# Tiles of every 64th node in a two-layer graph attention kernel, with eight columns to take out the diagonal

## The chip, the core and the metric

The kernel runs on one core of a Trainium2 chip. The metric is the device time of one execution in microseconds (us). "Before" is the kernel ahead of the change, "after" the kernel behind it. Engines: TensorE (PE), VectorE (DVE), ScalarE (ACT), GpSimd (POOL), and SyncE (SP), which here only issues DMAs. The core's 16 DMA engines move all data between DRAM and SBUF.

## The reference

There are N = 8192 nodes with D = 128 features each, and an adjacency matrix of 8192 x 8192 int32 (256 MiB) that holds the diagonal and some 8 other neighbours in a row.

```python
h = jnp.maximum(_layernorm(x), 0.0)
x = x + _L0_gnn_ref(h, adj, W, a)
h = jnp.maximum(_layernorm(x), 0.0)
x = x + _L1_gnn_ref(h, adj, Wq, bq, Wk, bk, Wv, bv)
...
# layer 0: s1 = (h@W)@a1, s2 = (h@W)@a2; e = leaky_relu(s1[:, None] + s2[None, :], 0.2)
#          out = elu(softmax(where(adj > 0, e, -9e15)) @ (h@W))
# layer 1: q, k, v = h@Wq.T+bq, h@Wk.T+bk, h@Wv.T+bv
#          out = elu(softmax(where(adj > 0, q@k.T/sqrt(128), -9e15)) @ v)
```

## The kernel before

The nodes are cut into T = 64 tiles of P = 128 nodes, one node for each SBUF partition. Tile t holds nodes 128 t to 128 t + 127. Each layer visits the tiles in turn.

**Start.** SP issues four loads of x (L445, 16 tiles each), the weights, and then adjacency tiles 0 and 1. ACT issues a load of the 8192 diagonal elements (L1169). DVE builds constants (L614 to L637), PE mixes weights (L1340 to L1346), DVE takes the statistics of all 64 tiles of x (L662), and during the first three tiles ACT, PE and DVE compute the projected rows h@W. POOL writes them, two tiles at a time, to a DRAM table, `table0` (L561).

**Layer 0 (`survey`).** For each tile, SP loads four quarters of 128 rows x 2048 columns (`load_adj`, L448), 1 MiB each, into one of two buffers. A quarter of tile t + 2 is issued when ACT has read the same quarter of tile t. ACT turns int32 into a bf16 mask (`read_quarter`, L1176). PE packs the 8192 columns into 512 PSUM columns with 16 matmuls, one for each segment of 512 columns, each by a multiple of the identity, `shifted[:, s, :]`, that holds 64 * 2^s (`pack`, L1354). `pack_end` takes out the node itself (L1360): in a tile of 128 nodes in a row, the diagonal elements lie in 128 neighbouring columns of one segment, and a 128 x 128 matrix `off_diag`, made by DVE's `hide_diag` (L637), is added there. DVE reads neighbours out of the packed sums (`extract`, L702), lists them (L761), and POOL gathers the neighbours' rows from `table0` with nine indirect DMAs for each tile (L574). A tile's own rows come by `load_self` (L461). Four to seven tiles later DVE and PE form scores, softmax and sums; the input of layer 1 is staged, and SP writes it four tiles at a time to `table1` (L482).

**Layer 1 (`attend`).** It does not read the adjacency again. For each tile, SP loads its own rows (L522), POOL gathers nine times from `table1` (L605), and SP writes `out` four tiles at a time (L515).

Engines run their instructions in program order and wait on semaphores. A branch that handles inputs which the lists can't hold is not taken.

Of the kernel before, what the change touches and what calls it, by code (L numbers as in the profile page):

```python
# [5 lines left out]
P = 128  # L6
# [35 lines left out]
def two_layer_graph_attention(nc, x, adj, W, a, Wq, bq, Wk, bk, Wv, bv, out):  # L42
# [15 lines left out]
    x_tiles = x.rearrange("(t p) d -> p t d", p=P)  # L58
    out_tiles = out.rearrange("(t p) d -> p t d", p=P)
# [3 lines left out]
    table1 = nc.dram_tensor("table1", [N + 1, D], F32, kind="Internal").ap()  # L63

    with ExitStack() as ctx:
# [111 lines left out]
        off_diag = place([2, P], BF16)  # L177
# [265 lines left out]
        def _(sp):  # L443
# [3 lines left out]
            def load_adj(tile, k, q):  # L447
                sp.dma_start(adj_sb[:, k, q, :], adj[bass.ds(tile * P, P), q * QUARTER:(q + 1) * QUARTER])\  # L448
                  .then_inc(adj_in[k][q], 16)
# [10 lines left out]
            def load_self(v, k):  # L460
                sp.dma_start(Gt[:, k, 0, :], table0[bass.ds(v * P + 1, P), :]).then_inc(self_in[k], 16)  # L461

            def load_group(g):
                for b in range(GROUP):
                    s = g * GROUP + b
                    if live(s, -2):
                        for q in range(QUARTERS):

                            sp.wait_ge(mask_done, QUARTERS * s + q + 1)
                            load_adj(s + 2, b % 2, q)  # L470
                    if isinstance(s, int) and s == 5:
                        sp.wait_ge(zeros_in, 32)
                        for k in range(4):
                            sp.wait_ge(table0_in[k], 16 * UNITS // 4)
                        load_self(0, 0)
                    if not isinstance(s, int) or 5 <= s < T + 4:

                        at_least(sp, summed, s - 7)
                        load_self(s - 4, b)
                    if b == 0 and (not isinstance(g, int) or 0 <= g - 4 < G):  # L480
                        sp.wait_ge(stage_done, (g - 3) * GROUP)
                        sp.dma_start(table1[1:N + 1, :].rearrange("(t p) d -> p t d", p=P)  # L482
                                     [:, bass.ds((g - 4) * GROUP, GROUP), :], stage[:, :, :]).then_inc(table1_in, 16)
# [5 lines left out]
            with sp.If(whole > 0):  # L489
# [4 lines left out]
                sp.dma_start(X[:, :, :], x_tiles).then_inc(w_x_again, 16)  # L494
# [13 lines left out]
                sp.dma_start(out_tiles, X[:, :, :]).then_inc(out_written, 16)  # L508
                sp.wait_ge(out_written, 16)
            with sp.Else():  # L510
# [7 lines left out]
                def own_rows(g):  # L518
                    for b in range(GROUP):
                        t = g * GROUP + b  # L520
                        sp.wait_ge(summed, T + t - 3)
                        sp.dma_start(Gt[:, b, 0, 0:D], table1[bass.ds(t * P + 1, P), :]).then_inc(self_in[b], 16)  # L522
                    if not isinstance(g, int) or g >= 2:
                        write_out(g - 2)
# [8 lines left out]
        def _(pool):  # L533
            small = dict(channel_multiplier=0, allow_small_or_imprecise_dtypes=True)
            scratch_u, scratch_p, scratch_q = hT[:, 0, 0:P], h_rows.rearrange("p a b d -> p (a b d)"), mine[:, 0, :]
# [12 lines left out]
            nc.gpsimd.memset(Gt[:, GROUP - 1, ROWS - 1, :], 0.0).then_inc(pool_consts, 1)  # L548
            nc.gpsimd.iota(iota_over[:, :], pattern=[[1, OVER]], base=0, **small).then_inc(pool_consts, 1)
# [5 lines left out]
            pool.wait_ge(pool_consts, 15)  # L555
# [3 lines left out]
            for i in range(UNITS):  # L559
                pool.wait_ge(wh_kept, i + 1)  # L560
                pool.dma_start(table0[1 + 2 * P * i:1 + 2 * P * (i + 1), :].rearrange("(t p) d -> p t d", p=P),  # L561
                               wh_rows[:, i % 4, :, :]).then_inc(table0_in[i % 4], 16)
# [48 lines left out]
        def _(dve):  # L611
            dve.wait_ge(consts_in, 16 * 9)
            dve.wait_ge(pool_consts, 15)
# [16 lines left out]
            DVE_CONSTS = 9 + SEGS  # L630
# [536 lines left out]
        def _(act):  # L1167
            flat = adj.rearrange("n m -> (n m)")
            act.dma_start(diag[:, :], flat[0:N * N:N + 1].rearrange("(t p) -> p t", p=P),  # L1169
                          allow_slow_non_contiguous=True).then_inc(diag_in, 16)  # L1170
            act.preload_act_table_set("natural_log_exp_and_others")
            act.wait_ge(pool_consts, 15)
# [159 lines left out]
        def _(pe):  # L1332
            pe.wait_ge(consts_in, 16 * 9)
            pe.wait_ge(pool_consts, 15)
# [12 lines left out]
            pe.wait_ge(dve_consts, 9 + SEGS)  # L1347
# [16 lines left out]
            pack_end(0, 0, 0, 0)  # L1364
# [40 lines left out]
            def survey(g):  # L1405
                for b in range(GROUP):
# [20 lines left out]
                    if live(t, -1):  # L1427
                        pack(t + 1, (b + 1) % 2, range(8, SEGS))
                        pack_end(t + 1, (b + 1) % 2, (b + 1) % GROUP, g + (b + 1) // GROUP)
# [132 lines left out]
```

## Time and profile before

| | us |
|---|---|
| Median of three runs | 2054.16 |
| Lowest and highest | 2051.19, 2054.91 |
| The profiled execution's own time | 2045.02 |
| Its span, first to last instruction | 2043.3 |
| PE busy | 1269.4 |
| DVE busy | 1285.6 |
| ACT busy | 768.5 |
| POOL busy | 1133.3 |

The page of the profile gives busy time of each engine, and what the DMA engines moved over the span. In the first half of the span (layer 0) they move 280 to 340 GB/s, in the second (layer 1) about 53 GB/s. A share of the span says little about a bound; waits within one stage say more.

### The profile page before, as it was taken

The numbers are of one execution on the slowest core, as the hardware profiler recorded it, in microseconds if no ns is written. First come the engines' busy times: TensorE is split into PE (matmuls) and PEld (weight loads), VectorE is DVE, ScalarE is ACT, GpSimd is POOL, SyncE is SP. The second block draws the span as 40 slices with busy tenths as digits, with TensorE's granted clock in tenths as the row PEclk, the third lists the DMA queues.
The fourth block names the chain that finished last, engine by engine and source line by source line (L and its number), as shares of the span: only waits on it lengthen the run. The fifth ranks groups of instructions, "written<-read, shape, count | busy, mean of one in ns | idle before, by whom it ended". The sixth has DMA issues, their size and how long they took to land.

```text
span 2043.3 us, 23565 instructions
## 1 busy us (share of the span) xinstructions
PE 1269.4 (62%) x5314; PEld 979.3 (48%) x5362; DVE 1285.6 (63%) x6912; ACT 768.5 (38%) x1507; POOL 1133.3 (55%) x1206
## 2 busy tenths in 40 slices
PE   2756766866567677667653356665666655666566
PEld 1433444444344444344443245655655555665555
DVE  4556777776777777777775255655555555555555
ACT  2865566666556656666621011111111111111111
POOL 1345655556455555555563656666666666666661
PEclk9876676677677766677755565556556666566665
DMA  9788999999799998899721211222221222222121
GB/s 311 290 308 320 326 324 327 325 321 317 280 327 319 325 324 312 318 340 323 240 55 38 57 42 50 53 54 52 55 53 52 55 53 53 54 53 52 48 55 31
DMA packets 122266, 372.43 MB, mean 182 GB/s; under 512 B 34577, under 2 KB 67858, under 8 KB 89362
## 3 DMA queue, kind: packets, MB, share of 16 engines
q1 hardware_dynamic: 75458, 289.83, 38.6%
q0 software_dynamic: 38464, 81.08, 15.4%
q10 hardware_dynamic: 8208, 0.03, 0.2%
q8 instruction: 46, 0.75, 0.2%
q14 instruction: 90, 0.74, 0.1%
HBM read 358.12 MB, written 12.72 MB: 181 GB/s over the span
## 4 chain that ended last, share of the span: by engine, by line
DVE 38%; another core or an unknown queue 30%; PE 10%; issue 7%; ACT 6%; DMA 4%; POOL 2%; SPq 1%; DVEq 1%; ACTq 0%; POOLq 0%
DVE arena L877 6%; PE psum L1394 3%; DMA arena<-table,arena 3%; DVE arena L702 3%; DVE arena L761 2%; ACT arena L1176 2%; POOL arena L574 2%; DVE arena L764 2%; PE psum L1531 2%; DVE arena L794 2%; PE psum L1532 2%; DMA table<-arena 1%; PE psum L1535 1%; DVE arena L1125 1%
## 5 line engine op out<-in xcount | busy, mean ns | idle before, releaser
L574 POOL DMA_INDIRECT arena<-table,arena x576 | 550.6, 956 | 434.2 <-issue 417.6
L605 POOL DMA_INDIRECT arena<-table,arena x576 | 554.4, 963 | 333.7 <-DVE arena L886 166.1
L1176 ACT ACTIVATE arena<-arena 128x2048 bf16<-128x2048 int32 x256 | 485.4, 1896 | 26.3 <-DMA arena<-in_adj_dram 26.2
L1354 PE MATMUL psum<-arena 128*128 128x512 bf16 x976 | 331.7, 484 | 111.8 <-ACT arena L1176 58.2
L1401 PE MATMUL psum<-arena 128*128 128x131 f32 (+1 forms) x768 | 205.7, 439 | 289.2 <-DVE arena L870 242.5
L1401 PEld LDWEIGHTS psum<-arena 128*128 128x128 f32 x768 | 171.5, 321 | 304.9 <-issue 304.4
L877 DVE SCALAR_TENSOR_TENSOR arena<-arena 128x131 f32<-128x131 f32 (+1 forms) x768 | 267.9, 349 | 42.2 <-DVE arena L877 16.9
L1354 PEld LDWEIGHTS psum<-arena 128*128 128x128 bf16 x1024 | 116.2, 123 | 281.1 <-issue 168.2
L1311 ACT ACTIVATE arena<-psum 128x384 f32<-128x384 f32 x64 | 31.5, 492 | 542.0 <-remote 510.7
L1387 PEld LDWEIGHTS psum<-arena 128*128 128x128 f32 x768 | 153.5, 289 | 58.7 <-DVE arena L842 48.9
L1394 PEld LDWEIGHTS psum<-arena 128*128 128x128 f32 x768 | 152.7, 280 | 60.4 <-DVE arena L860 42.0
L1387 PE MATMUL psum<-arena 128*128 128x18 f32 x768 | 147.4, 326 | 53.5 <-DVE arena L842 45.4
L1531 PE MATMUL psum<-arena 128*128 128x128 f32 x128 | 50.5, 498 | 207.3 <-ACT arena L1318 197.3
L1394 PE MATMUL psum<-arena 128*128 128x1 f32 x768 | 140.5, 298 | 41.7 <-DVE arena L860 36.2
L864 DVE TENSOR_TENSOR arena<-arena,psum 128x3 f32<-128x3 f32 x128 | 19.7, 154 | 228.7 <-remote 102.9
L1225 ACT ACTIVATE arena<-psum 128x465 f32<-128x465 f32 x64 | 35.7, 558 | 305.5 <-PE psum L1418 147.9
L1531 PEld LDWEIGHTS psum<-arena 128*128 128x128 f32 x128 | 31.9, 309 | 214.2 <-ACT arena L1318 203.4
L1418 PE MATMUL psum<-arena 128*128 128x155 f32 x384 | 119.1, 481 | 3.3 <-DVE arena L794 1.8
L858 DVE TENSOR_TENSOR arena<-psum,arena 128x18 f32<-128x18 f32 x128 | 22.3, 174 | 152.3 <-remote 149.9
L1520 PE MATMUL psum<-arena 128*128 128x128 f32 x384 | 117.1, 407 | 1.0 <-issue 1.0
L1521 PE MATMUL psum<-arena 128*128 128x129 f32 x384 | 113.7, 394 | 0.0
L1125 DVE SCALAR_TENSOR_TENSOR arena<-arena 128x129 f32<-128x129 f32 x448 | 102.3, 291 | 9.5 <-DMA arena<-table,arena 5.6
(199 smaller groups left out, 2241.9 us busy)
## 6 DMA issues: line engine op xcount, KB each, us to landing
arena<-in_adj_dram SPq DMA_DIRECT2D x256, 1024.0 KB
arena<-table,arena POOLq DMA_INDIRECT x1152
table<-arena POOLq DMA_DIRECT2D x32, 132.0 KB, 5.2
arena<-table SPq DMA_DIRECT2D x64, 66.0 KB
table<-arena SPq DMA_DIRECT2D x16, 256.0 KB
arena<-table SPq DMA_DIRECT2D x64, 64.0 KB
out_dram<-arena SPq DMA_DIRECT2D x16, 256.0 KB
arena<-in_x_dram SPq DMA_DIRECT2D x4, 0.5 KB, 12.1
```

The costliest lines, as they stand in the source:

```text
L574: pool.indirect_dma_start(Gt[:, v % GROUP, c + 1, :], None, table0, bass.IndirectOffsetOnAxis(idx_now[:, v % GROUP, c:c + 1], 0))\
L605: pool.indirect_dma_start(Gt[:, t % GROUP, c + 1, 0:D], None, table1, bass.IndirectOffsetOnAxis(idx_now[:, t % GROUP, c:c + 1], 0))\
L877: nc.vector.scalar_tensor_tensor(out=acc_sb[:, k, 0:width], in0=Gt[:, r, c, 0:width], scalar=p10[:, k, c:c + 1], in1=acc_sb[:, k, 0:width] ...
L1125: nc.vector.scalar_tensor_tensor(out=prod[:, c, :], in0=Gt[:, b, c, 0:DE], scalar=SCALE, in1=u_row[:, b, P:], op0=ALU.mult, op1=ALU.mult, ...
L1176: nc.scalar.activation(mask[:, k, q * QUARTER:(q + 1) * QUARTER], adj_sb[:, k, q, :], ACT.Relu, accum_out=sum_all[:, bass.ds(tile, 1), q:q ...
L1354: nc.tensor.matmul(V[k], shifted[:, s, :], mask[:, k, s * 512:(s + 1) * 512], start=(s == 0), stop=False)
L1387: last = nc.tensor.matmul(by_slot_ps[k], owned[:, r, c, :], slot_e[:, k, c, :], start=(c == 0), stop=(c == CHUNKS - 1))
L1394: last = nc.tensor.matmul(max_ps[k][:, c:c + 1], mine[:, r, c * P:(c + 1) * P], neg_max[:, k, :], start=True, stop=True)
L1401: last = nc.tensor.matmul(acc_ps[k][:, 0:width], weighted[:, c, :], Gt[:, r, OWN + c, 0:width], start=(c == 0), stop=(c == CHUNKS - 1))
L1418: last = nc.tensor.matmul(deal_ps[v % 2][:, c, :], mine[:, v % GROUP, c * P:(c + 1) * P], dealt[:, v % GROUP, :], start=True, stop=True)
L1520: nc.tensor.matmul(own_ps[m][:, c, :], mine_c, ident[:, :], start=True, stop=True)
L1531: nc.tensor.matmul(o_ps[k], accT[:, k, :], proj[:, 1, :], start=True, stop=False)
```

## The change

A tile now holds nodes t, 64 + t, 128 + t and so on: partition p holds node 64 p + t. So partition p of x, of both tables and of `out` is a run of 64 whole rows in DRAM, and a transfer of n tiles moves n rows in one run. For the adjacency matrix, the 128 rows of a tile now lie 64 rows apart (64 x 32 KiB = 2 MiB) where they lay 32 KiB apart; a quarter is still 128 runs of 8 KiB. The diagonal elements of a tile fall into 8 columns of each of the 16 segments. The 128 x 8 matrix `off_diag` is made from `which8`, and a new constant `own_shift` gives each partition the weight of its own segment. Both are built once, at the start, from a pattern by POOL and some twenty DVE instructions.

```diff
-    x_tiles = x.rearrange("(t p) d -> p t d", p=P)
-    out_tiles = out.rearrange("(t p) d -> p t d", p=P)
+    x_tiles = x.rearrange("(p t) d -> p t d", p=P)
+    out_tiles = out.rearrange("(p t) d -> p t d", p=P)
+    adj_rows = adj.rearrange("(p t) m -> p t m", p=P)
...
+    rows0 = table0[1:N + 1, :].rearrange("(p t) d -> p t d", p=P)
+    rows1 = table1[1:N + 1, :].rearrange("(p t) d -> p t d", p=P)
...
-        off_diag = place([2, P], BF16)
+        off_diag = place([2, 8], BF16)
+        which8 = place([8], BF16)
+        own_shift = place([P], BF16)
...
             def load_adj(tile, k, q):
-                sp.dma_start(adj_sb[:, k, q, :], adj[bass.ds(tile * P, P), q * QUARTER:(q + 1) * QUARTER])\
+                sp.dma_start(adj_sb[:, k, q:q + 1, :], adj_rows[:, bass.ds(tile, 1), q * QUARTER:(q + 1) * QUARTER])\
...
             def load_self(v, k):
-                sp.dma_start(Gt[:, k, 0, :], table0[bass.ds(v * P + 1, P), :]).then_inc(self_in[k], 16)
+                sp.dma_start(Gt[:, k, 0:1, :], rows0[:, bass.ds(v, 1), :]).then_inc(self_in[k], 16)
...
-                        sp.dma_start(table1[1:N + 1, :].rearrange("(t p) d -> p t d", p=P)
-                                     [:, bass.ds((g - 4) * GROUP, GROUP), :], stage[:, :, :]).then_inc(table1_in, 16)
+                        sp.dma_start(rows1[:, bass.ds((g - 4) * GROUP, GROUP), :], stage[:, :, :]).then_inc(table1_in, 16)
...
-                        sp.dma_start(Gt[:, b, 0, 0:D], table1[bass.ds(t * P + 1, P), :]).then_inc(self_in[b], 16)
+                        sp.dma_start(Gt[:, b, 0:1, 0:D], rows1[:, bass.ds(t, 1), :]).then_inc(self_in[b], 16)
...
+            by16 = hT[:, 1, 0:P]
+            nc.gpsimd.affine_select(out=by16, in_=ones[:, 0:P], compare_op=ALU.is_equal, fill=0.0, base=0,
+                                    pattern=[[-8, 16], [-1, 8]], channel_multiplier=1).then_inc(pool_consts, 1)
...
-                pool.dma_start(table0[1 + 2 * P * i:1 + 2 * P * (i + 1), :].rearrange("(t p) d -> p t d", p=P),
-                               wh_rows[:, i % 4, :, :]).then_inc(table0_in[i % 4], 16)
+                pool.dma_start(rows0[:, 2 * i:2 * i + 2, :], wh_rows[:, i % 4, :, :]).then_inc(table0_in[i % 4], 16)
...
-            DVE_CONSTS = 9 + SEGS
+            by16 = hT[:, 1, 0:P].rearrange("p (s c) -> p s c", s=SEGS)
+            in_seg = half_gap[:, 0:SEGS]
+            place8 = half_gap[:, SEGS:SEGS + 8]
+            nc.vector.tensor_reduce(place8, hT[:, 1, 0:P].rearrange("p (s c) -> p c s", s=SEGS), AX.X, ALU.add)\
+              .then_inc(dve_consts, 1)
+            nc.vector.tensor_reduce(in_seg, by16, AX.X, ALU.add).then_inc(dve_consts, 1)
+            dve.wait_ge(dve_consts, 11 + SEGS)
+            nc.vector.tensor_copy(which8[:, :], place8).then_inc(dve_consts, 1)
+            nc.vector.tensor_scalar(own_shift[:, :], shifted[:, 0, :], in_seg[:, 0:1], None, ALU.mult).then_inc(dve_consts, 1)
+            for n in range(1, SEGS):
+                dve.wait_ge(dve_consts, 12 + SEGS + n)
+                nc.vector.scalar_tensor_tensor(out=own_shift[:, :], in0=shifted[:, n, :], scalar=in_seg[:, n:n + 1],
+                                               in1=own_shift[:, :], op0=ALU.mult, op1=ALU.add).then_inc(dve_consts, 1)
+            DVE_CONSTS = 12 + 2 * SEGS
...
             def hide_diag(tile, k):
-                nc.vector.tensor_scalar(off_diag[:, k, :], ident16[:, :], neg_diag[:, bass.ds(tile, 1)], None, ALU.mult)\
+                nc.vector.tensor_scalar(off_diag[:, k, :], which8[:, :], neg_diag[:, bass.ds(tile, 1)], None, ALU.mult)\
...
-            act.dma_start(diag[:, :], flat[0:N * N:N + 1].rearrange("(t p) -> p t", p=P),
+            act.dma_start(diag[:, :], flat[0:N * N:N + 1].rearrange("(p t) -> p t", p=P),
...
-            def pack_end(tile, k, n, seg):
+            def pack_end(tile, k):
                 pe.wait_ge(off_done, tile + 1)
-                hide = shifted[:, seg, :] if isinstance(seg, int) else \
-                    shifted[:, bass.ds(seg, 1), :].rearrange("p o d -> p (o d)")
-                nc.tensor.matmul(V[k][:, n * P:(n + 1) * P], hide, off_diag[:, k, :], start=False, stop=False)
+                nc.tensor.matmul(V[k][:, tile:512:T], own_shift[:, :], off_diag[:, k, :], start=False, stop=False)
```

On DVE's queue at the start, between the 16 `shifted` constants (L628 before, L638 after) and the statistics of x, the order before was this (name of line, operation, shape of the output, and how often in a row):

```order
L628 TENSOR_SCALAR arena<-arena 128x128 x16
L632 TENSOR_SCALAR arena<-arena 128x64
L633 TENSOR_SCALAR arena<-arena 128x64
L637 TENSOR_SCALAR arena<-arena 128x128
L643 COPY arena<-psum 128x256
```

And after:

```order
L638 TENSOR_SCALAR arena<-arena 128x128 x16
L644 TENSOR_REDUCE arena<-arena 128x8
L646 TENSOR_REDUCE arena<-arena 128x16
L648 CAST arena<-arena 128x8
L649 TENSOR_SCALAR arena<-arena 128x128
L652 SCALAR_TENSOR_TENSOR arena<-arena 128x128 x15
L656 TENSOR_SCALAR arena<-arena 128x64
L657 TENSOR_SCALAR arena<-arena 128x64
L661 TENSOR_SCALAR arena<-arena 128x8
L667 COPY arena<-psum 128x256
```

Nineteen instructions now stand ahead of the copy that PE's weight mixing waits for (L643 before, L667 after), and `hide_diag` (L637, L661) writes 8 columns in place of 128.

On SP's queue, the head before was:

```order
L445 DMA arena<-in_x_dram 128x16x128 x4
L452 DMA arena<-in_L_gnn_W_dram 128x128
...
L448 DMA arena<-in_adj_dram 128x2048 x32
L461 DMA arena<-table 128x132 x2
```

And after:

```order
L454 DMA arena<-in_x_dram 128x2048 x4
L461 DMA arena<-in_L_gnn_W_dram 128x128
...
L457 DMA arena<-in_adj_dram 128x2048 x32
L470 DMA arena<-table 128x132 x2
```

The order is the same. A load of x is now 128 runs of 2048 elements where it was 128 x 16 runs of 128; adjacency loads keep their shape.

## Rows read from the trace of the kernel before

**Rows 1.** The page: span, and busy time of each engine.

```profile
span 2043.3 us, 23565 instructions
PE 1269.4 (62%) x5314; PEld 979.3 (48%) x5362; DVE 1285.6 (63%) x6912; ACT 768.5 (38%) x1507; POOL 1133.3 (55%) x1206
```

**Rows 2.** Windows, one in each layer: busy of engines, PE's clock, DMA share, GB/s.

```profile
400.00:900.00 500.00, 338.24 (x1342) 220.62 (x1367) 365.60 (x1975) 308.11 (x467) 275.76 (x290) 0.69 0.91 318
1200.00:1900.00 700.00, 436.62 (x1924) 401.39 (x1922) 397.99 (x2175) 99.36 (x404) 439.47 (x457) 0.59 0.21 53
```

**Rows 3.** DMA queues, 400 to 900 us: packets, MB, share of 16 engines; issues.

```profile
q1 hardware_dynamic: 27499, 139.17, 75.3%
q0 software_dynamic: 9248, 19.55, 15.2%
...
arena<-in_adj_dram SPq DMA_DIRECT2D x129, 1024.0 KB
```

**Rows 4.** SP's waits, 60 to 1000 us: total us, times, longest.

```profile
SPq L448 <- ACT arena L1176: 351.5, 132, 16.8
```

**Rows 5.** Waits of the engines, 60 to 1000 us, two of the longest.

```profile
ACT arena L1225 <- PE psum L1418: 147.9, 35, 14.5
...
DVE arena L864 <- remote: 87.8, 27, 4.5
```

**Rows 6.** DMA queues, 0 to 22 us (loads of x, and the diagonal on q10).

```profile
q1 hardware_dynamic: 2506, 4.37, 76.3%
q10 hardware_dynamic: 8208, 0.03, 22.5%
```

**Rows 7.** DMA queues, 30 to 50 us (adjacency alone).

```profile
DMA packets 1153, 8.40 MB, mean 420 GB/s; under 512 B 128, under 2 KB 128, under 8 KB 128
...
q1 hardware_dynamic: 1152, 8.39, 101.3%
```

**Rows 8.** Timeline of the start: start us, duration us, engine, line, idle before.

```profile
0.88 13.69 SPq L445 DMA_DIRECT2D arena<-in_x_dram  x4
14.62 4.06 SPq L452 DMA_DIRECT2D arena<-in_L_gnn_W_dram  x1
...
24.11 0.29 DVE L614 TENSOR_SCALAR arena<-arena 128x128 f32<-128x128 f32 x1 [24.11 <-DMA arena<-in_L_gnn_bv_dram]
...
26.22 2.25 DVE L628 TENSOR_SCALAR arena<-arena 128x128 bf16<-128x128 f32 x16
...
28.89 0.42 DVE L643 COPY arena<-psum 128x256 f32<-128x256 f32 x1
...
34.95 12.46 DVE L662 BATCH_NORM_STATS2 arena<-arena 128x6 f32<-128x128 f32 x64
...
48.51 0.35 ACT L1190 ACTIVATE arena<-arena 128x64 f32<-128x64 f32 x1 [11.78 <-DVE arena L671]
```

**Rows 9.** Groups by line: operation, shapes, count, busy us, mean ns.

```profile
L637 DVE TENSOR_SCALAR arena<-arena 128x128 bf16<-128x128 bf16 x64 | 19.4, 302 | 0.0
...
L1360 PE MATMUL psum<-arena 128*128 128x128 bf16 x64 | 15.6, 244 | 0.1
...
L826 DVE TENSOR_REDUCE arena<-arena 128x3 f32<-128x54 f32 x64 | 13.0, 203 | 0.0
...
L832 DVE TENSOR_SCALAR arena<-arena 128x25 bf16<-128x25 f32 x64 | 11.3, 176 | 0.0
```

**Rows 10.** Timeline near 444 us, three DVE instructions that wait for each other.

```profile
444.02 0.29 DVE L895 SCALAR_TENSOR_TENSOR arena<-arena 128x128 f32<-128x128 f32 x1
444.35 0.29 DVE L898 SCALAR_TENSOR_TENSOR arena<-arena 128x128 f32<-128x128 f32 x1
...
444.68 0.29 DVE L903 BATCH_NORM_STATS2 arena<-arena 128x6 f32<-128x128 f32 x1
```

**Rows 11.** DMA queues, 22 to 50 us (the fullest stretch).

```profile
q1 hardware_dynamic: 2256, 11.03, 98.4%
```

**Rows 12.** DMA queues, 1200 to 1900 us (gathers of layer 1).

```profile
q0 software_dynamic: 14624, 29.98, 17.2%
```

**Rows 13.** Timeline, end of the program: the last write of `out`.

```profile
2040.58 0.39 SPq L515 DMA_DIRECT2D out_dram<-arena  x1
```

More of the change, by code:

```diff
@@ L56, in two_layer_graph_attention @@
     QUARTER = N // QUARTERS
-    x_tiles = x.rearrange("(t p) d -> p t d", p=P)
-    out_tiles = out.rearrange("(t p) d -> p t d", p=P)
+    x_tiles = x.rearrange("(p t) d -> p t d", p=P)
+    out_tiles = out.rearrange("(p t) d -> p t d", p=P)
+    x_blocks = x.rearrange("(t p) d -> p t d", p=P)
+    out_blocks = out.rearrange("(t p) d -> p t d", p=P)
+    adj_rows = adj.rearrange("(p t) m -> p t m", p=P)
     col = lambda v: v.rearrange("(p o) -> p o", o=1)
@@ L493, in _ @@
                 sp.wait_ge(table1_in, 16 * G)
-                sp.dma_start(X[:, :, :], x_tiles).then_inc(w_x_again, 16)
+                sp.dma_start(X[:, :, :], x_blocks).then_inc(w_x_again, 16)
                 for layer in range(2):
@@ L507, in _ @@
                 sp.wait_ge(w_x_done, 2 * T)
-                sp.dma_start(out_tiles, X[:, :, :]).then_inc(out_written, 16)
+                sp.dma_start(out_blocks, X[:, :, :]).then_inc(out_written, 16)
                 sp.wait_ge(out_written, 16)
@@ L554, in _ @@
                            allow_small_or_imprecise_dtypes=True).then_inc(pool_consts, 1)
-            pool.wait_ge(pool_consts, 15)
+            pool.wait_ge(pool_consts, 16)
             pool.dma_start(table0[0:1, :], zeros).then_inc(zeros_in, 16)
@@ L612, in _ @@
             dve.wait_ge(consts_in, 16 * 9)
-            dve.wait_ge(pool_consts, 15)
+            dve.wait_ge(pool_consts, 16)
             nc.vector.tensor_scalar(spread[:, 0, :], ones[:, 0:D], bq_c, None, ALU.mult).then_inc(spread_done, 1)
@@ L1168, in _ @@
             flat = adj.rearrange("n m -> (n m)")
-            act.dma_start(diag[:, :], flat[0:N * N:N + 1].rearrange("(t p) -> p t", p=P),
+            act.dma_start(diag[:, :], flat[0:N * N:N + 1].rearrange("(p t) -> p t", p=P),
                           allow_slow_non_contiguous=True).then_inc(diag_in, 16)
             act.preload_act_table_set("natural_log_exp_and_others")
-            act.wait_ge(pool_consts, 15)
+            act.wait_ge(pool_consts, 16)
             def read_quarter(tile, k, q, nth):
@@ L1333, in _ @@
             pe.wait_ge(consts_in, 16 * 9)
-            pe.wait_ge(pool_consts, 15)
+            pe.wait_ge(pool_consts, 16)
             nc.tensor.transpose(bank(2)[:, 0:D], w_sb, ident[:, :]).then_inc(w_turned, 1)
@@ L1346, in _ @@
             nc.tensor.matmul(bank(5)[:, 0:DE], spread[:, 0, :], wk_bk[:, :], start=True, stop=True).then_inc(mixed, 1)
-            pe.wait_ge(dve_consts, 9 + SEGS)
+            pe.wait_ge(dve_consts, 12 + 2 * SEGS)
             def pack(tile, k, segments):
@@ L1354, in pack @@
                     nc.tensor.matmul(V[k], shifted[:, s, :], mask[:, k, s * 512:(s + 1) * 512], start=(s == 0), stop=False)
-            def pack_end(tile, k, n, seg):
+            def pack_end(tile, k):
                 pe.wait_ge(off_done, tile + 1)
-                hide = shifted[:, seg, :] if isinstance(seg, int) else \
-                    shifted[:, bass.ds(seg, 1), :].rearrange("p o d -> p (o d)")
-                nc.tensor.matmul(V[k][:, n * P:(n + 1) * P], hide, off_diag[:, k, :], start=False, stop=False)
+                nc.tensor.matmul(V[k][:, tile:512:T], own_shift[:, :], off_diag[:, k, :], start=False, stop=False)
                 nc.tensor.matmul(V[k], ones16[0:1, :], place16[0:1, :], start=False, stop=True).then_inc(packed, 1)
             pack(0, 0, range(SEGS))
-            pack_end(0, 0, 0, 0)
+            pack_end(0, 0)
             pe.wait_ge(mixed_sb, 12)
@@ L1428, in survey @@
                         pack(t + 1, (b + 1) % 2, range(8, SEGS))
-                        pack_end(t + 1, (b + 1) % 2, (b + 1) % GROUP, g + (b + 1) // GROUP)
+                        pack_end(t + 1, (b + 1) % 2)
                     if t < 3:
```

## The prediction

> **What bounds the kernel now.** I read the page first: no engine is busy for more than 63% of the span [rows 1], so the question is what each stage waits for. The windows split the run: in layer 0 the DMA engines are 91% busy and move 318 GB/s, in layer 1 21% and 53 GB/s [rows 2]. Layer 1 can hardly feel a change in how DRAM is laid out.
>
> In layer 0, 129 quarters are issued in 500 us [rows 3], that is 32.25 tiles, a period of 15.5 us. Two things in the waits tell what sets it. SP's queue waits for ACT to free a buffer, 351.5 us in 132 waits [rows 4]: the loads are asked for as early as two buffers allow, and they arrive in time, for ACT waits for PE's dealing matmuls and DVE for results of PE, not for adjacency [rows 5]. So the loop ACT, PE, DVE sets the period, and the DMA engines follow with about 9% to spare. The reader is to see how thin this margin is: 90.5% of 15.5 us is 14.0 us of DMA work for each tile [rows 3], of 15.3 us that can be had if the engines are never fuller than the 98.4% of their fullest stretch [rows 11]. The slack is 1.2 us a tile, under a tenth.
>
> **The change part by part.**
>
> *Loads of x.* In the first 22 us q1 moves 4.37 MB in 76.3% of the time, 16.8 us; the diagonal takes 22.5% beside it [rows 6]. With runs of 8 KiB, 32 KiB from one partition to the next, x has the very form of today's adjacency loads, which move 420 GB/s [rows 7]: 4.19 MB in 10.0 us. All behind it, the small weights first, comes 6.8 us earlier, and SP's issues, which now stand for 13.7 and 4.1 us because a load has 2048 runs [rows 8], are short. The constants that DVE starts on at 24.11 us [rows 8] land near 17.3.
>
> *New constants on DVE.* Two reductions at some 0.25 us (0.203 for a smaller one), a cast at 0.18 [rows 9], one multiplication at 0.14 (16 take 2.25 us [rows 8]), and 15 instructions each waiting for the one before: such a chain steps by 0.33 us [rows 10], 5.0 in all. With a wait more, 5.9 us. Queued behind them is the copy at 28.89 us, for which PE's weight mixing waits, then the statistics at 34.95, then ACT's root at 48.51 after 11.78 us of idleness [rows 8]. So the path through the start gains 6.8 and loses 5.9: -0.9 us. The bounds: -3 if the chain steps by its 0.2 us of work, +5.9 if the constants land no earlier. POOL's additional pattern lies in front of 14 us in which nobody waits for it.
>
> *Eight columns.* `hide_diag` goes from 302 ns to that of a small instruction, 176 [rows 9]: 0.13 us a tile. It is on the path where DVE is, so between 0 and -8.1 us over 64 tiles; I take half, -4. PE's matmul goes from 244 ns [rows 9] to something under it; loading 128 x 128 weights stays, and PE has idle time around it: 0, at most -3.
>
> *Tables and `out`.* Each is written in longer runs, but the work is small: x with runs of 512 bytes shows 260 GB/s (4.37 MB in 16.8 us), so a 256 KB store is 1.0 us of DMA and may become 0.6. Only the last, issued at 2040.58 [rows 13], has nobody to hide it: -0.3. For each four tiles of layer 0 the stores of `table1` lower the DMA work by 0.1 us a tile. Own rows (`load_self`, L522) keep 128 runs each and are needed tiles later: 0.
>
> *Adjacency.* Same bytes, same 8 KiB runs, same issues; what changes is that the rows that the 16 engines read at one time lie multiples of 2 MiB apart, and so agree in far more address bits than now. If memory is divided among its parts by the lower address bits, they all fall on the same part at the same time. No row of this trace has such a load, so I bound it. At best nothing: 420 GB/s, 10.0 us of the 14.0 a tile [rows 7]. At worst the rate at which rows scattered over DRAM are read now: the gathers of layer 1 take 17.2% of 700 us for 29.98 MB [rows 12], 249 GB/s, so 16.8 us a tile, +6.8. Two rows speak for the better end. The 512-byte runs of x reach 260 GB/s though they are in order, so most of the gathers' slowness is the size of a piece. And the diagonal is read in 8208 packets, elements about 4 MiB apart one after the other, at 22.5% x 22 us x 16 / 8208 = 10 ns each [rows 6]; but they are no power of two apart (512 bytes more), and they carry no bytes to speak of. For the worse end speaks that nothing else in the kernel asks of DRAM what this load would. I take the middle of the two rates, 335 GB/s: 12.5 us, +2.5. Then a tile needs 14.0 - 0.1 + 2.5 = 16.4 us of DMA, and at 98.4% full a period of 16.7, which is 1.2 above today's. The steady part runs from about 120 to 1000 us, 57 tiles: +68 us. While the DMA engines are the bound, the gain of `hide_diag` is hidden.
>
> The Trainium skill has a rule on just this, in "DMA: Bandwidth & Descriptors", section "Latency and other measured facts": copies of 128-partition tiles between DRAM tensors slow down when the rows of neighbouring partitions lie a large power of two apart, from 214 GB/s at full rate to 164 at 2 MiB and 103 at 4 MiB. No run here shows it yet, and those are copies from DRAM to DRAM with rows of 16 KiB. By its ratio, 0.77, an adjacency tile would take 10.0 / 0.77 = 13.0 us, the period (13.9 + 3.0) / 0.984 = 17.2, and the kernel would end at about 2155; by its bare 164 GB/s the tile would take 25.6 us, and the kernel near 2900.
>
> **The sum.** The profiled execution took 2045.02 us, 1.7 over its span of 2043.3; the median of three is 2054.16, so what I add goes on 2054. Start -0.9, last store -0.3: 2053. Adjacency +68, and 6 to 8 us for the first tiles, where the engines are full anyway (11.03 MB in 28 us [rows 11]: about 24 us of adjacency by a quarter slower). I forecast **2128 us**.
>
> **The rivals.**
>
> *A: the rows' distance costs nothing, or less than the slack.* Then the sum is 2054 - 0.9 - 4 - 0.3 = 2049, between 2038 and 2058 by the bounds above. It holds as long as a tile's adjacency takes under 10.0 + 1.3 us, that is above 371 GB/s. [...] Against it: how thin the slack is. This is the rival on the other side: the start and DVE's shorter instruction then decide.
>
> *B (the forecast): the DMA engines become the bound of layer 0*, with 250 to 371 GB/s for adjacency: from 2058 to, at the worst rate, (13.9 + 6.8) / 0.984 = 21.0 us a tile, +5.5 x 57 = +315 and some 12 at the start, 2380.
>
> *C: it falls under the rate of the gathers*, since there pieces are scattered over all of memory and here they might all meet in one part of it. At half the gathers' rate, 34 us a tile, the kernel would take over 3000 us; anything above 2380 is this case.
>
> *D: the start gets longer.* If x shares the DMA engines with the diagonal so that nothing lands earlier, the new chain is bare: +5.9, which with A gives 2055 to 2058. It decides only if A holds.
>
> **How the numbers follow.** B 0.50, A 0.38, D 0.04, C 0.08. A run of this kernel can be told from no change by about 0.2%, 4 us. Of A, two thirds lie more than that below 2054; so faster 0.26, same 0.15 (the rest of A, and part of D), slower 0.59. The range has to hold A's lower bound and B's upper: 2036 to 2380, which leaves out C and a little of each end. B's own range is 2070 to 2300.
>
> **What would show it.** In the profile after, windows between 400 and 900 us: B right if the DMA share there is 0.97 or more with GB/s under 318, the adjacency issues in 500 us number about 119, and ACT's mask (L1176 before) waits for in_adj_dram, which it hardly does now. A right if 129 or more are issued, at a share near 0.9. In the stretch of adjacency alone near 30 to 50 us the rate itself can be read: 420 or less. For the start: DVE's first constant near 17 us in place of 24.11, the chain of 15 taking 5 us, the statistics starting near 34. `hide_diag` at about 170 ns. The prediction is wrong if adjacency keeps 420 GB/s with packets from 2 MiB apart, or if the loop of engines has become so tied to late loads that a small loss of rate costs several us a tile.

## The result, and the profile after

| | before | after |
|---|---|---|
| Median, us | 2054.16 | 2104.12 |
| Lowest and highest of five | 2051.19, 2054.91 | 2098.8, 2110.94 |
| Span of the profiled execution | 2043.3 | 2097.1 |

The ratio is 1.0264, 95% interval 1.0236 to 1.0293: 2.6% slower, inside the range and on the side that was forecast, 24 us under the forecast of 2128. The reasons have to be looked at one by one, for the sum came out nearer than its terms did. The term for the steady part was 57 us too large and the terms for what lies ahead of it 38 us too small; that they nearly cancel is luck.

The DMA queues of the profile after, from 400 to 900 us, the stretch of [rows 3]:

```profile
q1 hardware_dynamic: 24066, 137.82, 86.8%
q0 software_dynamic: 9131, 19.30, 12.4%
...
arena<-in_adj_dram SPq DMA_DIRECT2D x126, 1024.0 KB
```

The two queues together now fill 99.2% of 16 engines, where they filled 90.5%, and move less. So the DMA engines did become full. But 126 quarters were issued against 129: 15.9 us a tile and not 16.7.

Rows of one DVE instruction (the sum of a tile, L886 before, L910 after), for the 4th and the 64th tile of layer 0, show where the time went. Before:

```profile
222.98 0.28 DVE L886 TENSOR_TENSOR arena<-psum,arena 128x131 f32<-128x131 f32 x1
...
1118.79 0.29 DVE L886 TENSOR_TENSOR arena<-psum,arena 128x131 f32<-128x131 f32 x1
```

After:

```profile
266.92 0.28 DVE L910 TENSOR_TENSOR arena<-psum,arena 128x131 f32<-128x131 f32 x1
...
1173.91 0.29 DVE L910 TENSOR_TENSOR arena<-psum,arena 128x131 f32<-128x131 f32 x1
```

The 4th tile's sum comes 43.9 us later. From there to the 64th it takes 907.0 us against 895.8, 11.2 more. What follows is 1.3 us shorter. These three make the 53.8 us between the spans. Four fifths of the loss arose before layer 0 had got going, where the forecast had put -0.9 for the start and 6 to 8 us for the first tiles.

The timeline of the start after, answering to [rows 8]:

```profile
0.82 2.15 SPq L454 DMA_DIRECT2D arena<-in_x_dram  x4
...
10.52 24.15 SPq L457 DMA_DIRECT2D arena<-in_adj_dram  x12
16.29 0.29 DVE L624 TENSOR_SCALAR arena<-arena 128x128 f32<-128x128 f32 x1 [16.29 <-DMA arena<-in_L_gnn_bv_dram]
...
20.57 0.37 DVE L644 TENSOR_REDUCE arena<-arena 128x8 f32<-128x128 f32 x1
...
21.53 5.78 DVE L652 SCALAR_TENSOR_TENSOR arena<-arena 128x128 bf16<-128x128 bf16 x15
...
63.57 0.20 DVE L656 TENSOR_SCALAR arena<-arena 128x64 f32<-128x64 int32 x1 [36.26 <-DMA arena<-in_adj_dram]
...
70.09 12.46 DVE L686 BATCH_NORM_STATS2 arena<-arena 128x6 f32<-128x128 f32 x64
```

The weights landed at 16.29 us (17.3 forecast), the new constants took 6.7 us (5.9 forecast). Then DVE stood for 36.26 us at the instruction that reads the diagonal, and all behind it began 35.1 us later than before, at 70.09 and not 34.95. The diagonal's load was issued at the same time as ever, but took 62.7 us to land, where it took 18.3. The DMA queues of the profile after, first from 0 to 22 us, then from 22 to 50, say why (q10 is the diagonal):

```profile
q1 hardware_dynamic: 2018, 6.62, 89.1%
q10 hardware_dynamic: 2481, 0.01, 6.5%
```

```profile
q1 hardware_dynamic: 1084, 7.88, 97.9%
q10 hardware_dynamic: 1085, 0.00, 2.2%
```

In the second pair there are 1084 packets of one queue and 1085 of the other. Before, all 8208 packets of the diagonal had gone by 22 us [rows 6]. Between 50 and 64 us the twelve adjacency loads that SP had been able to issue come to their end, and the diagonal's other 4642 packets go through:

```profile
q1 hardware_dynamic: 356, 2.54, 62.8%
q10 hardware_dynamic: 4642, 0.02, 18.6%
```

### The profile page after: what moved, and what is told of

Same layout as the page of the kernel before. It is cut to its first block, busy times and chain, and to the rows that moved or that the text cites. A ratio compares the mean times of both kernels' runs of the same rounds, so it can differ in the third digit from the quotient of the medians.

```text
span 2097.1 us, 23567 instructions
## 1 busy us (share of the span) xinstructions
PE 1281.3 (61%) x5314; PEld 977.6 (47%) x5362; DVE 1291.9 (62%) x6931; ACT 771.2 (37%) x1507; POOL 1126.8 (54%) x1207
## 3 DMA queue, kind: packets, MB, share of 16 engines
q0 software_dynamic: 38464, 81.08, 13.8%
q10 hardware_dynamic: 8208, 0.03, 0.2%
## 4 chain that ended last, share of the span: by engine, by line
DVE 38%; another core or an unknown queue 26%; PE 10%; DMA 10%; issue 8%; ACT 6%; POOL 1%; DVEq 0%; SPq 0%; ACTq 0%
DVE arena L901 8%; DMA arena<-table,arena 6%; ACT arena L1200 4%; PE psum L1416 4%; DVE arena L1149 3%; DVE arena L726 2%; DMA table<-arena 2%; DVE arena L785 2%; DVE arena L788 2%; DVE arena L818 1%; DVE arena L1153 1%; PE psum L1378 1%; POOL arena L584 1%; DMA arena<-in_adj_dram 1%
## 5 line engine op out<-in xcount | busy, mean ns | idle before, releaser
L1200 ACT ACTIVATE arena<-arena 128x2048 bf16<-128x2048 int32 x256 | 485.5, 1897 | 28.1 <-DMA arena<-in_adj_dram 27.6
L1378 PE MATMUL psum<-arena 128*128 128x512 bf16 x976 | 348.3, 504 | 118.0 <-issue 59.6
L1423 PEld LDWEIGHTS psum<-arena 128*128 128x128 f32 x768 | 170.5, 320 | 306.5 <-issue 298.6
L1416 PEld LDWEIGHTS psum<-arena 128*128 128x128 f32 x768 | 152.3, 279 | 126.5 <-DVE arena L884 97.8
L1416 PE MATMUL psum<-arena 128*128 128x1 f32 x768 | 145.3, 305 | 100.0 <-DVE arena L884 84.6
L1409 PEld LDWEIGHTS psum<-arena 128*128 128x128 f32 x768 | 153.2, 289 | 45.6 <-DVE arena L866 36.0
L1553 PE MATMUL psum<-arena 128*128 128x128 f32 x128 | 43.8, 438 | 152.6 <-ACT arena L1342 96.8
L1542 PE MATMUL psum<-arena 128*128 128x128 f32 x384 | 118.9, 412 | 1.0 <-DVE arena L1142 1.0
L1227 ACT ACTIVATE arena<-arena 128x7 f32<-128x7 f32 x128 | 37.9, 296 | 191.9 <-DVE arena L884 181.2
```

The source lines that it names most:

```text
L1200: nc.scalar.activation(mask[:, k, q * QUARTER:(q + 1) * QUARTER], adj_sb[:, k, q, :], ACT.Relu, accum_out=sum_all[:, bass.ds(tile, 1), q:q ...
L1378: nc.tensor.matmul(V[k], shifted[:, s, :], mask[:, k, s * 512:(s + 1) * 512], start=(s == 0), stop=False)
L1409: last = nc.tensor.matmul(by_slot_ps[k], owned[:, r, c, :], slot_e[:, k, c, :], start=(c == 0), stop=(c == CHUNKS - 1))
L1416: last = nc.tensor.matmul(max_ps[k][:, c:c + 1], mine[:, r, c * P:(c + 1) * P], neg_max[:, k, :], start=True, stop=True)
L1423: last = nc.tensor.matmul(acc_ps[k][:, 0:width], weighted[:, c, :], Gt[:, r, OWN + c, 0:width], start=(c == 0), stop=(c == CHUNKS - 1))
L1542: nc.tensor.matmul(own_ps[m][:, c, :], mine_c, ident[:, :], start=True, stop=True)
```

## The experiments

All ran on a chip on which the kernel before takes 1718 us and not 2054; each is compared with runs of before on that chip. (That it is another chip than the one of the result above is inferred from the times.) The instructions are the same there, and so, nearly, are their own times: ACT's mask takes 1895 ns on the first and 1897 on the second, `extract`'s MAX8 225 and 222. What differs is how soon one engine goes on after another, and the last section returns to it. Where a kernel's tiles compute with adjacency rows of other nodes, the lists differ a little, and that alone seems to be worth some microseconds: e8_rows_512k is the control for it. The trace of e7_diag_order, whose lists are right and whose time is that of before, stands for before on this chip.

**e1_gate.** After, with one wait.

```diff
+            sp.wait_ge(diag_in, 16)
             for n in range(2):
                 for q in range(QUARTERS):
                     load_adj(n, n, q)
```

> The kernel after, with one wait added: SP issues the first adjacency load only when the diagonal has landed. In the profile after, the diagonal landed 62.7 us after its issue (18.3 before) and DVE stood 36.3 us for it. Theory S (the start holds most of the loss: the diagonal's 4-byte packets alternate one for one with the 8 KiB packets of the adjacency, 802 to 803 packets between 30 and 50 us): the diagonal lands by about 25 us, the first statistics of x start near 34 us instead of 70, and the kernel takes about 2104 - 36 = 2068 us, ratio to before 1.007. Theory F (the far adjacency rows hold the loss in the steady part, as the prediction had it): the time stays above 2095, since the start is only a part of what the engines recover later.

Measured: 1950.3 us against 1717.7, ratio 1.134 (1.131 to 1.138). The start went as theory S had it: the diagonal landed after 18.3 us and the statistics began at 33.98. But the total fell outside both theories, since this chip charges far more for something else.

**e2_x_runs.** Before, with x alone in long runs.

```diff
-    x_tiles = x.rearrange("(t p) d -> p t d", p=P)
+    x_tiles = x.rearrange("(p t) d -> p t d", p=P)
```

> The kernel before, with the loads of x alone changed to 64 rows for each partition (runs of 8 KiB); nothing else moves, and the features thereby belong to other nodes. Adjacency rows stay 32 KiB apart, and the diagonal is read in the old order. Theory S, alternation: x no longer holds SP back, the adjacency reaches the DMA queues at about 10 us, the diagonal again lands only after 50 to 65 us and the kernel is 30 to 40 us slower, about 2088. Rival O, the diagonal's new order of reading is what made it slow: here it lands near 18 us, and the kernel is 5 us faster, about 2048.

Measured: 1739.8 us, ratio 1.013 (1.010 to 1.015), 22 us slower. The timeline:

```profile
49.08 0.20 DVE L632 TENSOR_SCALAR arena<-arena 128x64 f32<-128x64 int32 x1 [28.81 <-DMA arena<-in_adj_dram]
```

The old order of reading the diagonal and near adjacency rows, and still it is late (48.2 us to land): that x left the queue sooner is enough. O falls.

**e3_adj_far.** Before, with adjacency rows 2 MiB apart, and the flag that chooses the branch held at zero (`ALU.is_gt` against 1.0e9 in place of 0.5).

```diff
-                sp.dma_start(adj_sb[:, k, q, :], adj[bass.ds(tile * P, P), q * QUARTER:(q + 1) * QUARTER])\
+                sp.dma_start(adj_sb[:, k, q:q + 1, :], adj_rows[:, bass.ds(tile, 1), q * QUARTER:(q + 1) * QUARTER])\
```

> The kernel before, with the adjacency loads alone changed to rows 2 MiB apart. The tiles thereby hold rows of other nodes than their diagonal and features; the verdict on whether the lists hold the input is set to yes, so that the same branch runs. Theory F: the DMA engines fill up in layer 0 (share 0.98 or more from 400 to 900 us) and the kernel loses 60 us or more. Theory S: a loss only of the size that the profile after shows between the 4th and the 64th tile's sum, 907 us against 896, so 11 us and a little for the first two tiles: 2062 to 2072.

Measured: 1920.6 us, ratio 1.121 (1.115 to 1.127), 203 us slower: here theory F is right, far beyond its figure. Its DMA queues from 30 to 50 us, where the adjacency is alone as in [rows 7]:

```profile
DMA packets 675, 4.89 MB, mean 245 GB/s; under 512 B 78, under 2 KB 78, under 8 KB 78
...
q1 hardware_dynamic: 674, 4.88, 99.9%
```

245 GB/s for the same 8 KiB runs that move at 420 when they lie 32 KiB apart.

**e4_gate_near.** e1_gate with adjacency rows 32 KiB apart (and the flag held).

```diff
-    adj_rows = adj.rearrange("(p t) m -> p t m", p=P)
+    adj_near = adj.rearrange("(t p) m -> p t m", p=P)
```

> The kernel of e1_gate, with adjacency rows 32 KiB apart again (so that a tile computes with rows of other nodes than its diagonal and features; the branch is held as in e3_adj_far). Against e1_gate it prices the distance of rows alone. Theory S: 11 to 20 us less than e1_gate, about 2052, that is, no different from before; the 8 KiB packets near 30 to 50 us come at about 420 GB/s. Theory F: 40 us or more less than e1_gate. Third possibility, that the rows' distance costs nothing and the steady loss has another cause (stores in longer runs, PE's strided columns): the same time as e1_gate.

Measured: 1701.7 us, ratio 0.990 (0.988 to 0.993), 249 us less than e1_gate, and 418 GB/s between 30 and 50 us. The distance of the rows is all of e1_gate's loss. Without it and without the late diagonal, what is left of the change is no loss.

**e5_after.** The kernel after, unchanged, on this chip.

> The kernel after, unchanged, measured again beside the kernel before. On the chip of the first four experiments the kernel before takes 1718 us where it took 2054 in the measurement of the change, and the adjacency 2 MiB apart cost 203 us there (ratio 1.121), with the wait on the diagonal 1.134. Theory P (the penalty of far rows is what is left of it beyond the engines' own period): on a chip where the kernel before takes about 1718 us the kernel after takes about 1950 + 28 = 1975, ratio 1.15; on one where it takes 2054, the ratio is 1.026 again. Rival: the ratio is 1.026 on either, and e1_gate's ratio came from the added wait.

Measured: 1974.2 us, ratio 1.147 (1.145 to 1.149), where theory P had 1975. The theory's figure was e1_gate's time plus e2_x_runs' loss, so this shows that the late diagonal has its price beside far rows too: 24 us over e1_gate. Its windows, then those of e7_diag_order, with the columns of [rows 2]:

```profile
400.00:900.00 500.00, 313.22 (x1258) 191.73 (x1280) 346.09 (x1868) 287.94 (x436) 262.70 (x275) 0.66 0.97 296
```

```profile
400.00:900.00 500.00, 366.34 (x1597) 228.32 (x1625) 440.55 (x2362) 354.48 (x548) 331.08 (x348) 0.76 0.95 358
```

With far rows the DMA engines are 97% full and move 296 GB/s, and every engine gets less done in 500 us. From the 4th to the 64th sum it is 945.1 us (271.03 to 1216.16) against 751.9 (198.32 to 950.26): 15.8 us a tile against 12.5. What ACT waits for between 200 and 1000 us shows by which waits, here in e5_after and then in e7_diag_order:

```profile
ACT arena L1271 <- DMA table<-arena: 177.8, 10, 19.9
ACT arena L1200 <- DMA arena<-in_adj_dram: 121.1, 75, 4.6
```

```profile
ACT arena L1247 <- DMA table<-arena: 67.2, 12, 10.0
...
ACT arena L1176 <- DMA arena<-in_adj_dram: 0.2, 1, 0.2
```

So ACT does wait for adjacency here, but it waits longer for SP's stores to `table1` to land, so that the staging rows come free. Those stores are issued on the queue on which the adjacency loads stand. The same sums in e3_adj_far, then in e1_gate, both with far rows and a diagonal in time:

```profile
243.41 0.28 DVE L887 TENSOR_TENSOR arena<-psum,arena 128x131 f32<-128x131 f32 x1
...
1152.49 0.30 DVE L887 TENSOR_TENSOR arena<-psum,arena 128x131 f32<-128x131 f32 x1
```

```profile
245.67 0.28 DVE L911 TENSOR_TENSOR arena<-psum,arena 128x131 f32<-128x131 f32 x1
...
1187.50 0.29 DVE L911 TENSOR_TENSOR arena<-psum,arena 128x131 f32<-128x131 f32 x1
```

Far rows alone make the 4th sum 45 us later (243.41 against 198.32), before the steady part has begun. And from there on e1_gate takes 941.8 us where e3_adj_far takes 909.1. With near rows the rest of the change costs nothing in this part (747.4 us in e4_gate_near); with far rows something in it costs 33 us more, of which other lists may make some 5. Which part it is, was not tested.

**e6_x_gate.** e2_x_runs with the wait of e1_gate.

> The kernel of e2_x_runs (before, with x alone in runs of 8 KiB) with the wait of e1_gate: no adjacency load until the diagonal has landed. e2_x_runs took 22 us more than before, with DVE standing 28.8 us for a diagonal that landed after 48.2 us. Theory S: the diagonal lands near 18 us, the time is 25 to 30 us under e2_x_runs and 3 to 8 us under before, since what is left is the weights landing some 7 us earlier. Rival: x's fast loads themselves crowd out the diagonal, and the time stays above before.

Measured: 1711.9 us, ratio 0.996 (0.995 to 0.998): 28 us under e2_x_runs, 7 under before. The statistics start at 27.02 us. Theory S holds, with its sign and its size.

**e7_diag_order.** Before, with the diagonal read in the new order.

```diff
-            act.dma_start(diag[:, :], flat[0:N * N:N + 1].rearrange("(t p) -> p t", p=P),
+            act.dma_start(diag[:, :], flat[0:N * N:N + 1].rearrange("(p t) -> p t", p=P),
```

> The kernel before with the order in which the diagonal is read alone changed (each partition reads elements 32 KiB apart in place of 4 MiB); the diagonal's values thereby belong to other nodes, and the branch is held as in e3_adj_far. Theory S: it lands at 18 us as before, and the time is that of before within 0.3%. Rival O: the order of reading is part of what made it late, and it lands after 25 us or more.

Measured: 1718.7 us, ratio 0.9997 (0.9987 to 1.0007); it lands after 18.2 us. The order is worth nothing either way.

**v1_fours.** Before, with tiles of every fourth node of 512, and the wait.

```diff
+    four = lambda v: v.rearrange("(g p b) d -> p g b d", p=P, b=GROUP)
+    x_tiles, out_tiles, adj_rows = four(x), four(out), four(adj)
+    rows0, rows1 = four(table0[1:N + 1, :]), four(table1[1:N + 1, :])
...
-                nc.tensor.matmul(V[k][:, n * P:(n + 1) * P], hide, off_diag[:, k, :], start=False, stop=False)
+                nc.tensor.matmul(V[k][:, n:512:GROUP], hide, off_diag[:, k, :], start=False, stop=False)
```

> A version that keeps what helped and leaves what hurt: a tile holds every fourth node of 512, so that four rows of x, of the tables and of out form one run of 2 KiB, adjacency rows of a tile lie 128 KiB apart, and the diagonal falls into every fourth column of one segment, so that the old constants and the 128-column matmul serve; the adjacency waits for the diagonal. Theory: rows 128 KiB apart keep the full rate, near 420 GB/s between 30 and 50 us, and the kernel takes 2 to 10 us less than before. Rival: 128 KiB is already far enough to slow the reads, and it is slower by more than 20 us.

Measured: 1712.3 us, ratio 0.9965 (0.9954 to 0.9975), a small but clear gain, with 418 GB/s between 30 and 50 us.

**e8_rows_512k and e9_rows_1m.** Before, with an adjacency load's rows 512 KiB and 1 MiB apart (flag held). The first:

```diff
-                sp.dma_start(adj_sb[:, k, q, :], adj[bass.ds(tile * P, P), q * QUARTER:(q + 1) * QUARTER])\
+                sp.dma_start(adj_sb[:, k, q, :], adj[bass.ds(tile * 96, 16 * P), q * QUARTER:(q + 1) * QUARTER]
+                             .rearrange("(p c) m -> p c m", c=16)[:, 0, :]).then_inc(adj_in[k][q], 16)
```

> The kernel before with the 128 rows of an adjacency load 512 KiB apart (a load starts 96 rows further for each tile), so that it reads other rows than the tile's own; the branch is held as in e3_adj_far. Rows 2 MiB apart gave 245 GB/s between 30 and 50 us and a ratio of 1.121; rows 128 KiB apart, in v1_fours, 418 GB/s. Theory A (the more low address bits the rows share, the fewer parts of memory serve a load; the Trainium skill's table has hardly any loss at 512 KiB): 400 GB/s or more, ratio within 0.5% of 1. Rival (any distance beyond v1_fours' costs alike): 250 GB/s, ratio near 1.12.

> As e8_rows_512k, with the rows 1 MiB apart (a load starts 64 rows further for each tile). Theory A: between the two, 300 to 400 GB/s and a ratio of 1.01 to 1.08. Rival (one threshold at 2 MiB): as before, ratio 1.

Measured: 1709.4 us, ratio 0.994 (0.992 to 0.996), and 1725.4, ratio 1.004 (1.002 to 1.006). The queues between 30 and 50 us, at 512 KiB and then at 1 MiB:

```profile
DMA packets 1154, 8.41 MB, mean 421 GB/s; under 512 B 127, under 2 KB 127, under 8 KB 127
```

```profile
DMA packets 1146, 8.35 MB, mean 417 GB/s; under 512 B 127, under 2 KB 127, under 8 KB 127
```

At 512 KiB nothing is lost; that it is 9 us faster than before I put down to its other lists, and count as the offset of such kernels. The traces bear this out: behind the 64th sum, where no adjacency is read, e8_rows_512k takes 760.0 us and e7_diag_order 767.5. Against this offset 1 MiB costs 16 us (the lists of that kernel are others again, so some microseconds of this are open), and 2 MiB costs 211. The rate is lost between 1 and 2 MiB, which is the rival's one threshold and not theory A's slope of 300 to 400 GB/s. Against the same offset, e4_gate_near gains 7.7 us, hardly more than e6_x_gate's 7.

**e10_wide_hide.** e4_gate_near with `off_diag` made over 128 columns, of which PE reads 8.

> The kernel of e4_gate_near (after, adjacency rows 32 KiB apart, loads behind the diagonal; a tile computes with rows of other nodes than its diagonal) with off_diag made 128 columns wide again, of which PE uses the first 8, so that DVE's instruction has its old size. e4_gate_near took 1701.7 us. The prediction priced the narrow instruction at 0 to -8.1 us and took -4. If DVE is on the path, 1706 to 1710; if not, 1702.

Measured: 1705.3 us, ratio 0.992 (0.990 to 0.995), against 0.990 (0.988 to 0.993). The intervals overlap: not settled, and if there is a gain it is no more than a few microseconds. The instruction itself takes 289 ns in e10_wide_hide and 271 in e4_gate_near, which is 1.2 us over 64 tiles. Its row in the profile after is to be read beside its 302 ns in [rows 9]; PE's follows, 244 ns before:

```profile
L661 DVE TENSOR_SCALAR arena<-arena 128x8 bf16<-128x8 bf16 x64 | 18.0, 281 | 0.0
...
L1382 PE MATMUL psum<-arena 128*128 128x8 bf16 x64 | 12.0, 187 | 0.1
```

**v2_fours_early.** v1_fours with DVE's start reordered: `measure_x(k)` is the block of 16 statistics for one quarter of x.

```diff
+            measure_x(0)
+            measure_x(1)
+            dve.wait_ge(consts_in, 16 * 9)
...
+            measure_x(2)
+            measure_x(3)
             dve.wait_ge(mixed, 1)
```

> v1_fours (1712.3 us, ratio 0.9965) with DVE's start in another order: constants that need no load first, then the statistics of the first half of x, which has landed by then, and of the second half while PE mixes the weights. In v1_fours the statistics stand as one block of 12.5 us behind both, and ACT idles for their end. Theory: ACT's root comes some 10 us earlier and so does everything behind it, about 1702, ratio 0.991. Rival: the first tiles are held by the adjacency loads and PE's packing, and nothing is gained.

Measured: 1708.7 us, ratio 0.994 (0.992 to 0.997). It is faster than before and than after; against v1_fours the intervals overlap. The timeline of its start:

```profile
8.41 6.27 DVE L632 BATCH_NORM_STATS2 arena<-arena 128x6 f32<-128x128 f32 x32
...
25.56 1.91 ACT L1186 ACTIVATE arena<-arena 128x2048 bf16<-128x2048 int32 x1 [6.28 <-DMA arena<-in_adj_dram]
...
34.91 0.33 ACT L1200 ACTIVATE arena<-arena 128x64 f32<-128x64 f32 x1
```

ACT's root stands at 34.91 us, right behind the first tile's four masks, and it is these, which wait for the adjacency behind the diagonal, that hold it now. The theory's 10 us came to about 4.

## Why the prediction was right, and where it was not

**Side and size.** It said slower, with the DMA engines as the bound of layer 0 (B), 2128 us. It is slower by 50 us. Of the forecast's 74 us, 68 were the steady part's and 7 the first tiles'; of the 54 measured between the profiles, 11 are the steady part's and 44 stand ahead of it. Right was the name of one culprit, the far rows. Wrong was where they would be paid, and a second culprit, the late diagonal, had been priced at nothing.

**Loads of x: -6.8.** The weights landed 7.8 us sooner (16.29 against 24.11). Right as a term. Wrong was what it does to its neighbours, and this is the first step that failed: "the diagonal takes 22.5% beside it", taken as a share of time that stays. The diagonal is 8208 packets of 4 bytes, and what it costs is turns, not bytes. While SP was held back by x's 2048 runs a load, its own queue gave the diagonal turns to spare: 2506 packets to 8208 in 22 us [rows 6]. Once x was four short issues, the adjacency stood in the queue from 10.5 us on, and as long as it did, every 4-byte packet waited for one of 8 KiB: 1085 to 1084. The Trainium skill says in "DMA: Bandwidth & Descriptors", section "Queues, rings and completion order", that each engine goes round between its queues a packet at a time; the counts agree. e2_x_runs makes the wait with x alone, e6_x_gate and e1_gate take it away with one wait of SP. So the mechanism is shown.

It held the statistics for 35.1 us, but not all of this is its own. The diagonal is in when the queued adjacency has run out, and far rows run out later: on the second chip it landed after 48.2 us with near rows (e2_x_runs) and after 65.1 with far ones (e5_after). Rival D came near, but bounded it at +5.9, by the chain alone.

**First tiles: 6 to 8.** This is the second step that failed, by its size. The term took "about 24 us of adjacency by a quarter slower". But 54 quarters have been issued by the 4th sum, before and after alike, which is 135 us of adjacency at 420 GB/s. On the second chip the 4th sum comes 23 us later with the late diagonal alone (221.37 in e2_x_runs, against 198.32), 45 with far rows alone (e3_adj_far), and 73 with both (271.03 in e5_after); the wait on the diagonal gives back 25 of it (245.67 in e1_gate). So the 44 us by which it is later on the chip of the prediction can't be given to the diagonal, though its 35.1 us stand on the path: without it, far rows would have held the first tiles for part of the same time.

**New constants: +5.9.** 6.7 us; the 15 chained instructions took 5.8 of it (5.0). Hidden behind the late diagonal in the kernel after; in e1_gate nothing hides it, and the statistics start at 33.98 where e6_x_gate, without these constants, has 27.02.

**Adjacency: +2.5 us a tile, period 16.7.** Full engines (99.2%, forecast at least 97), 315 GB/s (under 318) and a longer period all appeared, but the period rose by 0.4 and not by 1.2. Redone with the queues of the profile after, the forecast's own sum shows where it was off. SP's queue (q1, nearly all of it adjacency) took 75.3% of 15.5 us a tile and takes 86.8% of 15.9: 13.8 us for 11.7, +2.1 where the forecast had +2.4. The gathers' queue (q0) took 15.2% and takes 12.4%: 0.4 us a tile less, where the forecast had no change. Together that is 15.7 us of DMA work and not 16.4. And the engines were filled to 99.2% and not to 98.4%. By this, two thirds of the 1.2 us fell away. (Between the 4th and the 64th sum it is less still, 0.2 us a tile.) Why the gathers' packets took less time is open.

The sign "ACT's mask waits for in_adj_dram" hardly appeared on the first chip (4.1 us in 4 waits from 200 to 1000 us) and did on the second (121.1 us in 75 waits).

The middle of two rates was a guess. Alone in its stretch, on the second chip, the true rate is the worst bound almost to the figure: 245 GB/s against the gathers' 249. In the steady part the same reads do better: in e5_after SP's queue moves 129.09 MB in 85.5% of 500 us, 302 GB/s of its own time.

```profile
q1 hardware_dynamic: 22517, 129.09, 85.5%
```

The start has a comparison that points at the reason. From 22 to 50 us e1_gate reads far rows alone, and e5_after reads them with a packet of the diagonal after each:

```profile
q1 hardware_dynamic: 933, 6.84, 99.2%
```

```profile
q1 hardware_dynamic: 1020, 7.42, 98.1%
```

8% more bytes move in the same time when another queue's packets come in between. That gathers do the same for the steady part fits this, but was not tested. On the first chip the kernel after moved 7.88 MB on this queue in this stretch, so 245 GB/s may be too low for far rows there.

What far rows cost is not one figure, then. From the 4th to the 64th sum a tile takes 15.1 us on the chip of the prediction, and on the other 15.2 (e3_adj_far), 15.7 (e1_gate) and 15.8 (e5_after). The engines' own period is 14.9 us on the first and 12.5 on the second. So the same change loses 11 us in this part on the one chip, and 193 on the other, mostly because the other has more to lose. Rival A's threshold, the slack of 1.2 us a tile, was the right question: it was nearly enough.

The Trainium skill's table on row pitch ("DMA: Bandwidth & Descriptors", section "Latency and other measured facts") had the side right: hardly any loss at 512 KiB, a loss at 2 MiB. For loads into SBUF in runs of 8 KiB, the loss at 2 MiB is larger than the table's ratio of 0.77: 245 / 420 = 0.58.

**Eight columns: -4, PE 0.** The narrow instruction takes 281 ns and not 176, so its price was -1.3 us at most. The step that failed is "that of a small instruction, 176": the row was another instruction's (L832, which reads f32), and only a row of `hide_diag` itself with few columns could have given the price. The same instruction with 128 and with 8 columns differs by 21 ns. PE's matmul gave 57 ns, unseen in the total.

**Tables and out.** As forecast, nothing to be seen there: the part behind the 64th sum is 1.3 us shorter. Whether the new places of the tables' rows are what costs e1_gate its 33 us against e3_adj_far is open.

## What to carry to other kernels

A load of many tiny packets is paid in turns, one for each large packet as long as such packets are queued beside it; whoever makes another queue quicker must ask who needs the tiny load first, and hold the large ones back until it is in. Before rows of a large matrix are dealt out to partitions at a power of two, look at how far apart they come to lie: up to 512 KiB cost nothing here, 1 MiB some 16 us, 2 MiB took 42% of the rate of a load alone. Count the tiles that are loaded before the steady part as well: there the DMA engines were the bound already. A change is worth what it moves the longer of two periods by, so its price is that of a chip too, and a kernel with slack on one may have none on the next.

## What was not expected of the hardware

The same kernel takes 2054 us on one chip and 1718 on another, both repeated within 0.3%. On the first, ACT's copy of layer 1 (L1311) waits 8.9 us and starts at 1622.22, when PE's last matmul for it (L1521), by its record, ended at 1618.38:

```profile
1617.78 0.60 PE L1521 MATMUL psum<-arena 128*128 128x129 f32 x2
...
1622.22 0.49 ACT L1311 ACTIVATE arena<-psum 128x384 f32<-128x384 f32 x1 [8.93 <-remote]
```

On the second the same pair, in e2_x_runs, follows at once:

```profile
1410.13 0.39 PE L1521 MATMUL psum<-arena 128*128 128x129 f32 x2
...
1410.56 0.49 ACT L1311 ACTIVATE arena<-psum 128x384 f32<-128x384 f32 x1 [4.90 <-PE psum L1521]
```

In this tile 3.8 us pass on one chip and none on the other. Over all 64 tiles ACT waits 542.0 us at this line on the first chip, 510.7 of them put down to "remote", which is to say that the view names no instruction as their releaser, and 315.2 us on the second, all put down to PE: 3.5 us a tile more, though not all of a wait need be a loss. The wait of DVE's L864 that [rows 5] shows as "remote" is of this kind too: on the second chip, in e7_diag_order, it is put down to PE's L1394. What stands between the engines on the first chip stays open, and no experiment ran on that chip. So the two mechanisms, turns and far rows, are shown by experiment on the second chip alone, and how the first chip's own 50 us divide between them rests on its two traces: 44 us by the 4th sum, where the two overlap, and 11 in the steady part, where only far rows are left.
